# Moving a sample's transposes and query projection from the middle of one sample's maxima pass to the end of the sample before

## The reference

```
x = normalise(x * s1)                         # per token, over the channels
q, k, v = (x @ Wq.T)*q_dc, (x @ Wk.T)*k_dc, (x @ Wv.T)*v_dc*s2      # 16 heads of 16 channels
attn = softmax(q @ k.T / 4)                   # per head, 256 x 256
out = (attn @ v) @ Ww.T * w_dc + v_flat @ Wu.T * u_dc
```

## Time and profile before

| | |
|---|---|
| median of 3 runs | 674.41 us (673.08 to 679.88) |
| profiled execution | 672.83 us, span 671.0 us |
| samples' part of the span | about 48 to 285 us |
| TensorE matmul busy | 495.6 us, 74% |
| VectorE busy | 490.5 us, 73% |
| ScalarE busy | 238.7 us, 36% |
| GpSimd busy | 163.2 us, 24% |
| granted TensorE clock, mean | 0.896 of full |

### The profile page before, as it was taken

The page is one execution under the profiler, slowest core; times in us unless marked ns, Lnnn a source line. Parts: engine busy times, 40 slices in busy tenths (PEclk is TensorE's granted clock), DMA queues, the critical chain, the costliest instruction groups (busy, mean ns, idle before and its releaser), DMA issues.

```text
span 671.0 us, 8832 instructions
## 1 busy us (share of the span) xinstructions
PE 495.6 (74%) x3238; PEld 291.5 (43%) x3256; DVE 490.5 (73%) x807; ACT 238.7 (36%) x488; POOL 163.2 (24%) x176
## 2 busy tenths in 40 slices
PE   2578988788888877999995210047787999999995
PEld 2454656464655643578885110001232333333333
DVE  2825868677686857547656789638796999999994
ACT  2332554535555350466675264500111111111111
POOL 5320022020201200084000034501242334334331
PEclk9875999999999997999998555558897999999999
DMA  9766061715436070004000045785674765766720
GB/s 362 232 118 118 1 118 25 143 39 104 83 61 124 20 142 0 2 1 188 1 1 0 16 157 217 250 112 98 93 111 82 112 107 116 113 105 118 112 54 23
DMA packets 42213, 65.13 MB, mean 97 GB/s; under 512 B 18327, under 2 KB 33047, under 8 KB 39178
## 3 DMA queue, kind: packets, MB, share of 16 engines
q1 hardware_dynamic: 41130, 61.36, 43.7%
q0 software_dynamic: 784, 3.15, 1.1%
q10 hardware_dynamic: 256, 0.07, 0.0%
HBM read 41.88 MB, written 22.61 MB: 96 GB/s over the span
## 4 chain that ended last, share of the span: by engine, by line
DVE 33%; PE 32%; DMA 17%; ACT 8%; issue 6%; POOL 2%; SPq 1%; DVEq 0%; ACTq 0%
DVE zring L1333 12%; DMA kst<-qk_d 8%; PE bank L694 6%; DVE acc L1195 6%; DMA xst<-xs_d 4%; PE bank L1001 4%; PE bank L962 4%; PE bank L973 4%; PE bank L713 4%; DVE mx L1135 3%; DMA qst<-mT 3%; ACT acc L562 2%; PE bank L750 2%; PE bank L723 2%; ACT xrp L557 2%
## 5 line engine op out<-in xcount | busy, mean ns | idle before, releaser
L1333 DVE CUSTOM_DVE_ANT_0 zring<-zring,bank,hi 128x512 f32<-128x512 f32 x192 | 143.6, 748 | 9.8 <-PE bank L962 3.1
L962 PE MATMUL bank<-xst,bst 128*128 128x512 bf16 x238 | 78.5, 401 | 74.1 <-DMA bst<-bd_d 46.9
L1135 DVE TENSOR_REDUCE mx<-bank 128x2 f32<-128x512 f32 x128 | 79.7, 684 | 12.4 <-PE bank L713 11.5
L962 PEld LDWEIGHTS bank<-xst,bst 128*128 128x128 bf16 x256 | 24.7, 99 | 123.4 <-issue 61.8
L522 ACT ACTIVATE ex<-bank 128x512 f32<-128x512 f32 x128 | 65.6, 645 | 26.1 <-PE bank L723 26.0
L973 PE MATMUL bank<-zring,cst 128*32 128x512 f32 x448 | 71.1, 629 | 1.1 <-DVE zlast L1333 1.1
L381 POOL TENSOR_TENSOR qk<-qk,part 128x512 f32<-128x512 f32 x16 | 19.6, 1230 | 186.7 <-ACT part L484 186.7
L1195 DVE SCALAR_TENSOR_TENSOR acc<-xrp,wcv,acc 128x256 f32<-128x256 f32 x96 | 40.1, 480 | 29.5 <-ACT acc L562 28.9
L1153 DVE TENSOR_TENSOR esum<-ex 128x1024 f32<-128x1024 f32 x32 | 39.1, 1222 | 28.8 <-ACT ex L522 28.3
L856 PE MATMUL bank<-xres,win 128*128 128x256 f32 x256 | 57.6, 382 | 1.4 <-ACT gateT L567 0.7
L694 PE MATMUL bank<-xnT,w 128*128 128x256 f32 x192 | 49.5, 407 | 4.8 <-ACT xnT L469 4.8
(11 more groups left out here) (168 smaller groups left out, 768.2 us busy)
## 6 DMA issues: line engine op xcount, KB each, us to landing
qk_d<-part SPq DMA_DIRECT2D x64, 96.0 KB, 2.5
xs_d<-xpart SPq DMA_DIRECT2D x16, 384.0 KB, 2.6
xst<-xs_d SPq DMA_DIRECT2D x15, 384.0 KB
xn_d<-xc SPq DMA_DIRECT2D x16, 256.0 KB, 2.8
xtk<-xn_d SPq DMA_DIRECT2D x64, 64.0 KB
xst<-xs_d SPq DMA_DIRECT2D x15, 256.0 KB
qst<-qk_d SPq DMA_DIRECT2D x8, 384.0 KB, 4.4
kst<-qk_d SPq DMA_DIRECT2D x8, 384.0 KB, 7.7
```

Of the source, the lines that this page charges most:

```text
L962: mm(bank[t % 4][:, :], bst[:, slot, t % RS, :], xst[:, slot, t % RS, :], start=True, stop=True)\
L1135: v.tensor_reduce(mx[:, :, HEADS[n]:HEADS[n] + 1], bank[4 + n % 4][:, :].rearrange("p (t k) -> p t k", t=HALVES), AX.X, ALU.max)\
L1333: v._custom_dve(bass.dve_ops.TENSOR_ADD_SAT, out=zst[t % ZR], in0=zst[(t - 1) % ZR], in1=bank[t % 4][:, :], s0=hi[:, t:t + 1], s1=0.0).the ...
```

## The change

The transposes, the wait for ScalarE's copy of them, and the q projection of sample b+2 are taken out of sample b+1's list, where they stood ahead of head 4. They are put at the end of sample b, behind `weigh(b, par, 3, False)` and ahead of `early_maxima(b+1)`. They are there in samples 0 to 5. Numbers on the semaphores are the same as before for the same sample. The k and v projections, and everything on the other engines, are left where they were.

```diff
-                def next_qkv(stage):
-...
-                    if stage == 0:
-                        transpose_xn(b + 1, first)
-                    elif stage == 1:
-                        pe.wait_ge(s["xnT_ready"], b + 2)
-                        if first:
-                            pe.wait_ge(s["q_in"], b + 1)
-                        channels_of(0, 1, "q_done")
-...
                 for n in range(EARLY, NH):
                     if first:
                         pass
-                    elif n == 4:
-                        next_qkv(0)
-                        next_qkv(1)
-                    elif n in (7, 10):
-                        next_qkv(2 if n == 7 else 3)
-                    elif not first and n == 14:
+                    elif n == 7 and not last:
+                        pe.wait_ge(s["att_ready"], b * 2)
+                        channels_of(1, 2, "k_done")
+                    elif n == 10 and not last:
+                        channels_of(2, 3, "vt_done")
+                    elif n == 14:
                         project_att(b - 1)
                     max_scores(b, par, n)
...
                 weigh(b, par, 2, True)
                 weigh(b, par, 3, False)
+                if b + 2 < B:
+                    transpose_xn(b + 2, False)
+                    pe.wait_ge(s["xnT_ready"], b + 3)
+                    channels_of(0, 1, "q_done")
                 if not last:
                     early_maxima(b + 1, 1 - par, next_turn)
                 weigh(b, par, 3, True)
```

More of the change, by code:

```diff
@@ L776, in sample @@
             def sample(b, par, next_turn, first, last):
-                def next_qkv(stage):
-                    if last:
-                        return
-                    if stage == 0:
-                        transpose_xn(b + 1, first)
-                    elif stage == 1:
-                        pe.wait_ge(s["xnT_ready"], b + 2)
-                        if first:
-                            pe.wait_ge(s["q_in"], b + 1)
-                        channels_of(0, 1, "q_done")
[L788 to L797, removed]
                 if first:
```

## The result

| | before | changed |
|---|---|---|
| median | 675.56 us (673.08 to 679.88, 4 runs) | 701.22 us (695.45 to 704.98, 4 runs) |
| ratio | | 1.0365, 95% interval 1.027 to 1.046 |
| profiled execution | 672.83 us, span 671.0 | 704.98 us, span 702.1 |
| granted clock, mean | 0.896 | 0.871 |

The kernel became slower, as forecast, but by 26 us where 20 were forecast; the range ended at 700. A second set of runs, beside the experiments, gave 698.76 against 677.18 us, ratio 1.0312 (1.0273 to 1.0351). Some executions of a kernel are in a slower state (7 of the 17 of the kernel before that ran beside the last experiment), and all medians and ratios here leave these out.

A forecast was written before the change was run, and what follows sets the result against it. Two almost equal loops, reload and attention, bound the kernel at 29.2 us per sample; 672.83 + 12.4 (k waiting for `attend(1)`) + 8.4 (clock) = 693.6, given as 694 us, range 684 to 700.

The forecast's parts named there:

- What bounds the kernel before: Samples 2 to 6: period 29.2 us, set by the reload loop, with the attention work only 1.3 us per sample behind.
- Two loops: Reload: early scores, k projection, store, `kst` landing; attention: early scores, maxima, exponentials, weighing; forecast 28.4 to 29.6 and 31.16 us.
- The moved block in its new place: Sample's end: early scores start 3.40 us behind the weighing of group 3, where before they started 1.32 behind.
- The k projection held by `attend(1)`: TensorE waits for `attend(1)`, so k starts 5.15 us behind the early scores; of 3.26 taken out, 0.16 come back.
- The sum without the clock: Samples 1 to 7: period goes from 29.20 to 31.16 us, sample 7's early scores come 12.4 us later (11.6 to 12.9).
- TensorE's clock: Ahead of k, clock falls in most of six samples, 1.4 us each, +8.4 us.
- the upper bound: Price of one clock fall: 6.8 us at half rate as in sample 7, all worked through, 3.4 us lost.
- B: Rival: the wait for `attend(1)` without a clock fall, 685.2 us, some 686 as a median; chance 0.17.
- C: Rival: not slower; `attT` there by about 2.65 us behind the early scores, loads hidden, 670 us; chance 0.04.
- D: Rival: clock stays low for long, 3.4 us in each of six samples, +20.4, 705.6 us; chance 0.10.

The follow-up runs named there:

- the last experiment: Kernel before with transposes at the sample's end, attend(1) and its weighing first, k straight behind q, v ahead of head 7; 672.35 against 678.25 us, ratio 0.9913.
- the filled kernel: Changed kernel plus four matmuls into free bank 0 ahead of the k projection's wait, result unread; 692.46 us against 679.05 of the kernel before, ratio 1.0190.
- the half change: Kernel before with only the transposes moved, copy wait and q projection kept ahead of head 4; 677.19 against 679.05 us, ratio 0.9983.
- the second profile: The changed kernel run again without further edits; 698.76 us against 677.18 of the kernel before, ratio 1.0312.
- `attend(1)` first: Changed kernel with the last sum weighing and attend(1) ahead of the early scores and early maxima; 676.92 us against 679.05 of the kernel before, ratio 0.9960.
- k into bank 0: Changed kernel with k of samples 2 to 7 in bank 0, v taking over the wait for attend(1); 680.60 us against 679.05 of the kernel before, ratio 1.0028.

## Why the prediction was wrong

- **What bounds the kernel before:** right. Two loops of nearly equal length, and the reload one hidden in the changed kernel up to sample 6; only sample 7 waits for `kst` again. Missing was a third bound close behind them, VectorE's own work between the early scores and the last maximum; it shows once `attend(1)` no longer holds k.
- **The moved block in its new place:** forecast 3.40 us from the weighing's end to the early scores; measured 111.25 less 107.83, 3.42. The first one is 3.40 late (78.49 for 75.09), forecast 3.50.
- **The k projection held by `attend(1)`:** forecast at 5.15 us behind the early scores, measured 5.15 (116.40 less 111.25) and the same in the filled kernel (179.57 less 174.42). Shown by moving `attend(1)`, by taking bank 2 out of it, and by the half change.
- **The sum without the clock:** forecast period 31.16, measured 31.24 and 31.15 where the clock stayed. Early scores of sample 1 at 78.49, five periods of 31.2 and the last period of 29.28, as the filled kernel has it without a fall, make 263.8 for sample 7, that is +12.6 us; forecast 12.4.
- **TensorE's clock: this step failed,** in its size. That it falls in most of the six samples while TensorE waits was right (six in one profile, four in the other; none at this place in the filled kernel). Its price was put at 1.4 us per sample, +8.4. A fall costs 1.6 or 2.8 us, and in the first profiled execution the clock took 12.4 in all (25.0 less 12.6; the fall in sample 6 cost only 1.2, 30.46 less 29.28, as the reload sets that period). I had priced the low stretch by the 3.6 us that were left of one in sample 0; in three of six samples it lasted 6.8 us, as in sample 7 of the kernel before, three quarters and more of it beside dense work, and in the other three 3.4 us. I had that row of sample 7 in hand as the upper bound, and set it aside for heads paced by VectorE. In the second profile the clock took 7.5 us, less than the 8.4; so the term also lacked the spread from one execution to the next.
- **What was left out:** sample 7 took 2.6 us more, with a second fall of the clock in it (what share of the 2.6 that has is not shown), and the second layer 3.5 us. The latter is within the scatter: from the first store of `bpart` to the end of the span the kernel before takes 233.7 us (671.0 less 437.33), the changed one 237.2, and the eight profiles of the experiments, with the same second layer, have 231.2 to 237.8. The profiled execution is thus 10.3 us above the sum: 0.2 from the wait, 4.0 from the clock, 2.6 and 3.5 from here. The range of 684 to 700 had 6 us above the forecast for all of this, and the clock's two prices, six times over, span 9.6 to 16.8 us. The first set's 701.22 is just outside the range, the second set's 698.76 inside it.
- **Rivals:** B (no fall) is nearly the filled kernel, +13.4 for a forecast of +12.4, with one fall elsewhere. C (not slower) had its place right, bank 2's wait, but not its number: with k into bank 0 it is +0.3%, since VectorE holds the later heads. D's 3.4 us per sample was never reached.

The page "TensorE: Matmul & The Clock Gate" of the Trainium skill, section "HAM oscillation — how this bites in real kernels", gives a limit for a single gap; the gap here, 2.3 us, is shorter, and the clock fell in ten of twelve cases. The same page of the Trainium skill has a section "A second HAM failure mode: psum-queue depth-cycling", where frequent short idle times drop the clock. The traces bear it out only in part: with `attend(1)` first heads 4 to 6 also stand ahead of k one by one, with 0.20 us of idle time before each, but without the 2.3 us, and the clock stayed at 1.00 in all six samples.

## What to carry to other kernels

A block that stands between two steps may be the cover of a wait that no view shows; before it is moved, ask what each later step on that engine waits for, and where the releasing step stands on the other engine's list. If it stands behind work that the moved block now delays, move the releasing step first. And price standing time of TensorE twice, once for itself and once for the clock: here the second was as large as the first in one execution (12.4 and 12.6 us) and smaller in another (7.5).

## What the runs showed of the hardware

- TensorE's clock fell in ten of twelve waits of 2.3 us, and each fall cost about 1.6 or 2.8 us, and 1.2 in one period that the reload set. The fall is not fixed by the code: with equal instruction order and equal waits (2.32 and 2.33 us) the same sample fell to 1.2 GHz in one execution and kept 2.4 GHz in another. It spreads the times: four executions of the changed kernel have spans of 693.7 to 702.1 us at mean clocks of 0.884 to 0.871.
- Matmuls whose result nobody reads, put into a wait of 2.3 us, made the kernel 8 to 12 us faster than without them.
- A fall can come behind the standing, in dense work: in the filled kernel at 130.6 us, 2 us behind a wait of 1.96 us for the row of maxima, with TensorE busy without a gap from 128.69 on.
